# Moving the choice of the two best experts from stage A's turns into stage B's attention iterations

## The reference

```
x = x + layernorm(mamba(layernorm(x)))            # stage A: scan over 512 steps, 16 states, 512 channels
x = x + layernorm(ffn(layernorm(x)))              # the layer below
  ffn(src):   src = src + moe_attn(src); src = ln1(src)
              src = src + relu(src @ W1 + b1) @ W2 + b2; src = ln2(src)
  moe_attn(x): 16 heads of 64, 8 experts a head
      q, k = rope(x Wq[h]), rope(x Wk[h])
      gv   = gate(x, Wsel_v);  v = sum_e gv[h,s,e] * (x Wv[h,e])
      o    = softmax(q k' / 8) v
      go   = gate(x, Wsel_o);  out = sum_{h,e} go[h,s,e] * (o Wo[h,e])
  gate(x, Wsel): s = sigmoid(x Wsel); keep the 2 largest of the 8 experts of a head, the others are 0
```

## Time and profile before

| | us |
|---|---|
| median of 3 runs (4547.19 to 4552.66) | 4552.34 |
| the profiled execution, its own time | 4550.93 |
| its span in the profile | 4549.1 |
| TensorE busy | 3873.6 |
| VectorE busy | 3483.8 |
| GpSimd busy | 2705.4 |
| ScalarE busy | 2037.9 |

### The profile page before, as it was taken

One profiled execution on the slowest core, in us unless ns is written; L12 is line 12 of the kernel. 1 busy time (PEld: TensorE's weight loads), 2 busy tenths in 40 slices (PEclk: granted clock), 3 DMA queues, 4 the chain that ended last, 5 costly groups with the idle time before them and its releaser, 6 DMA issues. The chain is left out here.

```text
span 4549.1 us, 52321 instructions
## 1 busy us (share of the span) xinstructions
PE 3873.6 (85%) x16256; PEld 2698.3 (59%) x16256; DVE 3483.8 (77%) x3612; ACT 2037.9 (45%) x3761; POOL 2705.4 (59%) x1772
## 2 busy tenths in 40 slices
PE   6776766857666399999999999999999999999787
PEld 2232322323222277777777777777777777777676
DVE  5999999999999566666666666666666666666598
ACT  4544534435343144444444444444544544444443
POOL 2756656566476365665665666656655755665454
PEclk7786777868776699999999999999999999999899
DMA  1000000000000210010010000000100100000001
GB/s 37 0 10 14 10 19 19 9 14 9 23 9 10 76 62 14 14 39 9 14 39 9 32 21 14 35 14 14 39 9 14 39 9 14 19 14 9 34 28 42
DMA packets 48726, 97.83 MB, mean 22 GB/s; under 512 B 3570, under 2 KB 33138, under 8 KB 46228
## 3 DMA queue, kind: packets, MB, share of 16 engines
q1 hardware_dynamic: 47620, 92.94, 5.8%
q0 software_dynamic: 1040, 4.19, 0.2%
HBM read 80.34 MB, written 16.78 MB: 21 GB/s over the span
## 5 line engine op out<-in xcount | busy, mean ns | idle before, releaser
L723 DVE TENSOR_TENSOR_SCAN state<-dA,dBx 128x2048 f32<-128x2048 f32 x128 | 706.5, 5519 | 9.3 <-POOL y_part L309 4.3
L1015 POOL TENSOR_TENSOR qk_full<-vg 128x512 f32<-128x512 f32 x256 | 329.9, 1289 | 455.6 <-DVE vg L1330 455.6
L1230 ACT ACTIVATE prob<-ps_b,negmax 128x512 f32<-128x512 f32 x512 | 346.1, 687 | 549.3 <-DVE negmax L1336 549.3
L306 POOL TENSOR_TENSOR state<-state,c_copy 128x1024 f32<-128x1024 f32 x120 | 302.0, 2516 | 420.6 <-DVE state L723 420.6
L396 PE MATMUL ps_a<-xp_high,ident_r 33*128 33x512 f32 x256 | 163.3, 638 | 425.1 <-DVE dBx L713 399.7
L1330 DVE TENSOR_TENSOR vg<-ps_b,gates 128x1024 f32<-128x1024 f32 x256 | 313.6, 1225 | 255.0 <-PE ps_b L1072 251.2
L573 ACT ACTIVATE dA<-dt,a_neg 128x511 f32<-128x511 f32 x512 | 326.9, 711 | 398.3 <-DVE state L723 397.9
L1029 POOL TENSOR_TENSOR ogT_low<-prob,ogT_high 128x512 fp32r<-128x512 f32 x256 | 322.0, 1287 | 201.6 <-ACT ogT_high L1261 201.6
L1070 PE MATMUL ps_b<-wv_high,xT_high 128*128 128x512 f32 x1024 | 414.2, 404 | 0.0
L1070 PE MATMUL ps_b<-ogT_high,wo_high 128*128 128x512 f32 x1024 | 408.4, 399 | 0.0
L396 PEld LDWEIGHTS ps_a<-xp_high,ident_r 33*128 33x128 f32 x256 | 59.5, 232 | 583.2 <-DVE dBx L713 488.6
(11 more groups left out here) (232 smaller groups left out, 9658.0 us busy)
## 6 DMA issues: line engine op xcount, KB each, us to landing
xT<-xT_scratch SPq DMA_DIRECT2D x65, 512.0 KB, 3.2
wv<-in_wv SPq DMA_DIRECT2D x8, 1024.0 KB, 4.9
wo<-in_wo SPq DMA_DIRECT2D x8, 1024.0 KB, 6.9
x_in<-in_x SPq DMA_DIRECT2D x8, 512.0 KB, 4.6
x_a<-in_x SPq DMA_DIRECT2D x8, 512.0 KB, 5.3
x_scratch<-x_a SPq DMA_DIRECT2D x8, 512.0 KB, 2.9
xT_scratch<-x2T SPq DMA_DIRECT2D x8, 512.0 KB, 2.6
gates_scratch<-gate SPq DMA_DIRECT2D x8, 512.0 KB, 3.5
```

What stands on the lines that cost most here:

```text
L723: dve.tensor_tensor_scan(h[n % 2][:, :, :].rearrange("p c s -> p (c s)"), dA[n % 2][:, :, :].rearrange("p c s -> p (c s)"), dBx[n % 2][:, ...
L1015: pool.tensor_tensor(v4[:, at, :, :], vg[:, at, 0:4, :], vg[:, at, 4:8, :], ALU.add).then_inc(vsum_done, 1)
L1230: act.activation(prob[h][:, t, :], ps[:, score_bank(t) + h, :], ACT.Exp, bias=negmax[:, t, h:h + 1], accum_out=total[:, h, t:t + 1]).then_ ...
```

## The change

Stage A ends its tail with the sigmoid, which now writes the scores in the order of the pairs; SP stores these scores (512 KB a batch, as the gates before). The selection code, its GpSimd part and four buffers leave stage A.

In stage B, SP loads the scores of a pair for all batches. Each iteration chooses the two best for the iteration that follows it (the first one is served in `start()`). The groups are now the 16 of one pair in four row blocks, 128 scores a partition. VectorE keeps the four maxima (`tops`, 128 elements each). The equality tests become a difference and a test against zero on GpSimd, in four functions with 14 instructions of 128 elements: `rank_one` (3), `rank_two` (4), `rank_three` (3), `rank_four` (4). They stand in GpSimd's queue ahead of the first value sum, ahead of the second (behind `low_wqk` where there is one), behind the first `low_values`, and behind `low_x`. `tops` 0 to 3 stand in VectorE's queue behind `gate_values` 0, `maxima` 1, `maxima` 2 and `gate_values` 3. `gates` becomes a single buffer for one iteration, written by the last instruction of `rank_four`. `sem_inc(held, 1)` counts a semaphore that nobody reads; it stands between a wait and the instruction behind it.

```diff
                 sp.dma_start(d["xT"][bass.ds(c, 1)].rearrange("b p k s -> p b k s"), x2T[:, :, :].unsqueeze(1)).then_inc(x2T_stored, 16)
-                sp.wait_ge(gate_done, CREDIT + c * TT + TT)
-                sp.dma_start(d["gates"][:, :, bass.ds(c, 1)].rearrange("j p b t c -> p b j (t c)"),
-                             gate[:, :, :, :].rearrange("p j t c -> p j (t c)").unsqueeze(1)).then_inc(gate_stored, 16)
+                sp.wait_ge(sg_done, CREDIT + c * 2 + 2)
+                sp.dma_start(d["scores"][:, :, bass.ds(c, 1)].rearrange("j p b t c -> p b j (t c)"),
+                             sg[:, :, :, :].rearrange("p j t c -> p j (t c)").unsqueeze(1)).then_inc(sg_stored, 16)
 
...
-
-            def rank_picked(c, k):
-                pool.wait_ge(top_step, c * TOP + k + 2)
-                pool.tensor_tensor(groups(rank), groups(pick), first_g, ALU.mult).then_inc(top_step, 1)
...
-                    if n in (11, 13) and has_tail:
-                        rank_picked(i - 1, 3 * (n - 11))
...
-            rank_picked(NB - 1, 0)
-            rank_picked(NB - 1, 6)
...
-                    act.wait_ge(gate_done, CREDIT + c * TT)
+                    act.wait_ge(x1_done, CREDIT + c)
...
             def sigmoid(c, half):
+                if half == 0:
+                    act.wait_ge(sg_stored, CREDIT + c * 16)
                 act.wait_ge(sel_psum, c * 2 + half + 1)
-                act.activation(sg[:, half * S:(half + 1) * S], ps[:, TAIL[half], :], ACT.Sigmoid).then_inc(sg_done, 1)
+                act.activation(sg[:, :, 2 * half:2 * half + 2, :].rearrange("p j t c -> p t j c"),
+                               ps[:, TAIL[half], :].rearrange("p (t j c) -> p t j c", t=2, j=PAIRS), ACT.Sigmoid).then_inc(sg_done, 1)
...
-            def best_of(c, src, k):
-
-                step = c * TOP + k
-                if k == 0:
-                    dve.wait_ge(sg_done, CREDIT + c * 2 + 2)
-                else:
-                    dve.wait_ge(top_step, step)
-                dve.tensor_reduce(best[:, :], groups(src), AX.X, ALU.max).then_inc(top_step, 1)
-                dve.wait_ge(top_step, step + 1)
-                dve.tensor_tensor(groups(pick), groups(src), best_e, ALU.is_equal).then_inc(top_step, 1)
-
-            def first_of(c, src, k):
-
-                step = c * TOP + k
-                dve.wait_ge(top_step, step + 3)
-                dve.tensor_reduce(best[:, :], groups(rank), AX.X, ALU.max).then_inc(top_step, 1)
-                dve.wait_ge(top_step, step + 4)
-                dve.tensor_tensor(groups(pick), groups(rank), best_e, ALU.is_equal).then_inc(top_step, 1)
-                dve.wait_ge(top_step, step + 5)
-                dve.scalar_tensor_tensor(left[:, :], pick, -2.0, src, ALU.mult, ALU.add).then_inc(top_step, 1)
-
-            def gates(c):
-                dve.wait_ge(top_step, c * TOP + TOP)
-                dve.wait_ge(gate_stored, CREDIT + c * 16)
-                for t in range(TT):
-                    dve.scalar_tensor_tensor(gate[:, :, t, :], by_pair(left, t), 0.0, by_pair(sg, t),
-                                             ALU.is_lt, ALU.mult).then_inc(gate_done, 1)
...
-                        elif n == 11:
-                            best_of(c, sg[:, :], 0)
-                        elif n == 12:
-                            first_of(c, sg[:, :], 0)
-                        elif n == 13:
-                            best_of(c, left[:, :], 6)
-                        elif n == 14:
-                            first_of(c, left[:, :], 6)
-                        elif n == 15:
-                            gates(c)
...
-            best_of(last, sg[:, :], 0)
-            first_of(last, sg[:, :], 0)
-            best_of(last, left[:, :], 6)
-            first_of(last, left[:, :], 6)
-            gates(last)
...
-        gates = sb("gates", [P, NB * TT, GP])
+        scores_in = sb("scores", [P, NB * TT, GP])
+        gates = sb("gates", [P, TT, GP])
+        first = sb("first", [P, E])
+        GROUPS = TT * GP // E
+        top, top_first = sb("top", [P, GROUPS]), sb("top_first", [P, GROUPS])
+        far, hit, rank, left, picked = (sb(n, [P, GROUPS, E]) for n in ("far", "hit", "rank", "left", "picked"))
...
-                sp.wait_ge(gate_step, CREDIT + j * NB * GATE)
-                sp.dma_start(gates[:, :, :].unsqueeze(1), d["gates"][bass.ds(j, 1)].rearrange("j p b t c -> p j (b t) c")).then_inc(gates_loaded, 16)
...
+                if more:
+                    sp.wait_ge(gates_done, j * NB + NB)
+                    load_scores(j + 1)
                 sp.wait_ge(xT_low, CREDIT + j * NB + NB)
                 load_xT(0)
 
+            def load_scores(j):
+                sp.dma_start(scores_in[:, :, :].unsqueeze(1), d["scores"][bass.ds(j, 1)].rearrange("j p b t c -> p j (b t) c")).then_inc(scores_loaded, 16)
...
             sp.dma_start(vg[:, 0:2, :, :].rearrange("p t e n -> p (t e n)"), d["spread"]).then_inc(consts_loaded, 16)
             load_xT(0)
+            sp.dma_start(first[:, :], d["first"]).then_inc(scores_loaded, 16)
+            load_scores(0)
             load_weights(0)
...
+            def above(it, step, k, src):
+
+                pool.wait_ge(top_done, CREDIT + it * TOPS + k + 1)
+                pool.sem_inc(held, 1)
+                pool.tensor_tensor(far[:, :, :], src, each(top), ALU.subtract).then_inc(rank_step, 1)
+                pool.wait_ge(rank_step, step + 1)
+                pool.sem_inc(held, 1)
+                pool.tensor_scalar(hit[:, :, :], far[:, :, :], 0.0, None, ALU.is_ge).then_inc(rank_step, 1)
+                pool.wait_ge(rank_step, step + 2)
+                pool.tensor_tensor(rank[:, :, :], hit[:, :, :], first_g, ALU.mult).then_inc(rank_step, 1)
+
+            def first_above(it, step, k):
+
+                pool.wait_ge(top_done, CREDIT + it * TOPS + k + 1)
+                pool.tensor_tensor(far[:, :, :], rank[:, :, :], each(top_first), ALU.subtract).then_inc(rank_step, 1)
+                pool.wait_ge(rank_step, step + 1)
+                pool.sem_inc(held, 1)
+
+            def rank_one(it, b):
+                above(it, CREDIT + it * RANK, 0, grouped(scores_in[:, bass.ds(b * TT, TT), :]))
+
+            def rank_two(it, b):
+                step = CREDIT + it * RANK + 3
+                first_above(it, step, 1)
+                pool.tensor_scalar(picked[:, :, :], far[:, :, :], 0.0, None, ALU.is_ge).then_inc(rank_step, 1)
+                pool.wait_ge(rank_step, step + 2)
+                pool.sem_inc(held, 1)
+                pool.tensor_scalar(hit[:, :, :], picked[:, :, :], -2.0, None, ALU.mult).then_inc(rank_step, 1)
+                pool.wait_ge(rank_step, step + 3)
+                pool.sem_inc(held, 1)
+                pool.tensor_tensor(left[:, :, :], hit[:, :, :], grouped(scores_in[:, bass.ds(b * TT, TT), :]), ALU.add).then_inc(rank_step, 1)
+
+            def rank_three(it):
+                above(it, CREDIT + it * RANK + 7, 2, left[:, :, :])
+
+            def rank_four(it, b):
+                step = CREDIT + it * RANK + 10
+                first_above(it, step, 3)
+                pool.tensor_scalar(hit[:, :, :], far[:, :, :], 0.0, None, ALU.is_ge).then_inc(rank_step, 1)
+                pool.wait_ge(rank_step, step + 2)
+                pool.tensor_tensor(picked[:, :, :], picked[:, :, :], hit[:, :, :], ALU.add).then_inc(rank_step, 1)
+                pool.wait_ge(rank_step, step + 3)
+                pool.wait_ge(gate_step, CREDIT + it * GATE)
+                pool.sem_inc(held, 1)
+                pool.tensor_tensor(grouped(gates[:, :, :]), picked[:, :, :], grouped(scores_in[:, bass.ds(b * TT, TT), :]), ALU.mult).then_inc(gates_done, 1)
+
             def start():
+                rank_one(0, 0)
+                rank_two(0, 0)
+                rank_three(0)
+                rank_four(0, 0)
                 low_wqk(0)
...
                 pool.wait_ge(qk_low, it + 1)
+                coming, ahead = more or more_pairs, b + 1 if more else 0
+                if coming:
+                    rank_one(it + 1, ahead)
                 sum_values(it, 0, 0)
                 if more_pairs:
                     low_wqk(j + 1)
+                if coming:
+                    rank_two(it + 1, ahead)
                 sum_values(it, 0, 1)
                 low_values(it, 0)
+                if coming:
+                    rank_three(it + 1)
                 sum_values(it, 1, 0)
                 sum_values(it, 1, 1)
                 low_values(it, 1)
                 low_x(it + 1)
+                if coming:
+                    rank_four(it + 1, ahead)
...
-                    dve.wait_ge(gates_loaded, j * 16 + 16)
+                    dve.wait_ge(gates_done, it + 1)
...
+            def top_of(it, k, src):
+
+                step = CREDIT + it * RANK
+                dve.wait_ge(rank_step, step + (0, 3, 7, 10)[k])
+                dve.tensor_reduce((top_first if k % 2 else top)[:, :], src, AX.X, ALU.max).then_inc(top_done, 1)
+
```

(38 more changed lines are left out.)

15 lines of the change are left out of this document (7 added, 8 removed).

## The result

The changed kernel took 4659.7 us (median of 4 runs, 4657.4 to 4661.8) against 4552.5 before (4 runs): ratio 1.024, 95% interval 1.022 to 1.026, 107 us slower. The forecast was 4610 (range 4525 to 4680), slower. The profiled execution took 4659.97 us with a span of 4658.2, 109.1 more than the span before.

The account below looks back on a forecast made before the run. VectorE was taken to bound stage A and TensorE stage B. Stage A gives back 117 us; stage B costs 16 + 151 + 9 = 176, so +59 on 4550.9 gives 4610 us, range 4525 to 4680.

Parts of the forecast that it names:

- upper end of my sum: The total if each GpSimd test takes 0.46 us, as a two-input operation: 3.0 us an iteration, +98, 4649 us.
- dear tests: Rival: GpSimd tests take a slower path, 1.29 us each, adding 4.0 us an iteration; about 4865 us, chance 0.10.
- my two signs of being wrong: Stage B's iteration period grows by less than 1.5 us, or GpSimd tests take over 0.5 us.
- Tests on GpSimd, 0.3 us each: Stage B: price of a one-input test or scaling of 128 elements, put between 0.13 and 0.46 us.
- The `held` increments, 0.04 us each: Stage B: price of each of seven semaphore increments in GpSimd's queue up to the last value sum; ends nothing and 0.1.
- 2.4 us an iteration: Stage B: 5.0 us added before GpSimd's last value sum, less 2.6 idle, reaches TensorE; 63 iterations, 151 us.
- Pair ends, 1.3 us each: Stage B: in seven iterations the low part of `wqk` stands before rank two and finds its idle time used; 9 us.
- Hidden work: rank four and the maxima: Stage B: rank four's 2 us lie behind GpSimd's wait for ScalarE; delays of VectorE's later maxima lie inside the 2.4.
- 14.4 us a turn in stage A: Time each of turns 1 to 6 gives back without the selection, not VectorE's 20.5; six turns, 86 us.
- The start, 16 us: Stage B's first TensorE product comes 16 us late, behind the score load, the first choice (8.7 us) and `low_wqk`.
- hidden in stage B: Rival: GpSimd's delay before its last value sum doesn't reach TensorE, only the start is paid; 4450 us, chance 0.20.
- Stage A gives all: Rival: seven turns of stage A give VectorE's full 20.5 us each, 162 and not 117; 4565 us, chance 0.10.

Follow-up runs that it names:

- run 28: Not a run label: 28 of 48 ordinary iterations in the changed kernel with two more GpSimd products ahead of the last value sum; that kernel took 4760.3 us.

## Why the prediction was right, and where its numbers were off

The sign and the mechanism were right: stage A's gain is smaller than what GpSimd's queue costs TensorE in stage B. The signs that I named for it are in the trace: TensorE's waits of 1.27 us for VectorE's low probabilities and 1.10 us behind it, and ScalarE's second value copy waiting for GpSimd, 3.77 us now. The time was 50 us over the forecast, and that it still fell into the range is in part luck. 4659.7 lies above the upper end of my sum, 4649, and under the 4865 of dear tests; only the range's stretch to 4680 holds it. The terms also erred both ways: stage A gave 14.5 us more than forecast, stage B and what follows cost 65 more. And of my two signs of being wrong one came true, tests over 0.5 us. It speaks against my price of a test and not against the mechanism, since the period grew by 3.06 us. These terms were mis-sized.

- **Tests on GpSimd, 0.3 us each.** They took 0.53, above my upper end of 0.46. Four in the chain: +0.9 us an iteration. The bound was wrong in kind: I took a two-input operation as the upper end for a one-input one. The Trainium skill (GPSIMD Engine Reference, section 4.1, Engine selection) has one-input operations at roughly line rate; at this size they were the dearer ones in the trace, 530 ns against 408 to 459, and what an element costs them can't be read from one size. Its 12 cycles an element for branches (section 3.1), the reason beside "dear tests", don't show in these tests: the multiplication by -2, which compares nothing, took 534 ns, as the tests did.
- **The `held` increments, 0.04 us each.** The gap is 0.20 and not 0.08 where one stands: 0.12 each, at the five places in the chain where one follows another GpSimd operation. It isn't the kind of operation: the addition at L1017 shows 0.19 with one, that at L1027 0.08 without. The seven gaps come to 1.14 us for 0.85; some 0.13 comes back, since what follows each of the three groups starts 0.04 us before its last operation ends.
- **The far differences, 0.46 us.** They took 0.41, three of them: -0.15 us.
- **2.4 us an iteration.** Ten operations, their gaps and the first maximum come to 3 x 0.41 + 3 x 0.46 + 4 x 0.53 + 1.14 - 0.13 + 0.28 = 6.0 us, not 5.0. Against them the idle times gave back 1.96 and 1.46 - 0.74, 2.7 us as forecast. The last sum is 3.3 late, the period 3.06: 63 x 3.06 = 193 us for 151. That the chain has no slack was right: 0.90 of 1.0 us put into it went to the period, and none of the same work behind it.
- **Pair ends, 1.3 us each.** The two iterations around a change of pairs took 47.87 and 45.07 us against 43.62 and 39.72, 3.5 us beyond two ordinary losses: 7 x 3.5 = 24 for 9. I had costed the low part of `wqk` alone. The next iteration, where GpSimd starts with the low output weights, was a catch-up of 2 us before and has none now.
- **Hidden work: rank four and the maxima.** Right in ordinary iterations: GpSimd's waits for ScalarE ahead of the low outputs fell from 3.16 to 0.60 us, and freeing the maxima of their waits left the shortest period at 44.80. At pair ends the cover isn't there, as the two products behind the low outputs showed (+1.0 us each time).
- **14.4 us a turn in stage A.** Six turns gave (1341.21 - 216.97) - (1238.90 - 213.95) = 99.3, 16.5 each, between my 14.4 and VectorE's 20.5. Turn 0, from which I took the limit, had a delay of its own: the same stretch takes 68.0 us before and 228.41 - 162.96 = 65.4 after, though neither has a selection there. Before, GpSimd waited 7.06 us for ScalarE's copy of `xp` and began its weighing at 163.76; after, at 160.75. With 65.4 as the limit my subtraction gives 17.0. The last turn gave 9.4 where I put 12: VectorE now waits 3.71 us for GpSimd's last sum ahead of the skip term, the wait that I had named but priced at 2. The tail gave 19.8 for 19, and turn 0 another 3.0, by that same delay. These 3 us aren't the change's: in the ten kernels with the new stage A turn 1 begins between 213.95 and 217.66, before it was 216.97.
- **The start, 16 us.** 18.2: from stage A's last store to the landing of `sin` it is 23.0 us, for which I had 22.1, and the chain took 9.9 us for 8.7, tests again.
- **Last iteration and stage C, nothing.** 5.4 us, of which 3.7 stand without a choice too.

Of the rivals, "hidden in stage B" was a matter of place. Its 4450 would need a free chain; with the choice in GpSimd's idle slots the kernel took 4486, on the faster side of before. "Stage A gives all" was a third true (131.5 us in the traces, between my 117 and its 162) and too small to decide. "Dear tests" had the right direction, with 0.53 us for its 1.29.

## What to carry to other kernels

Work moved to an engine that is two thirds busy costs what its place in that engine's queue costs: ten small operations cost 3.1 us an iteration in front of the value sums, and all 14 nothing in the slots where the engine waits for others, so look at the timeline for the idle time in front of a wait before choosing where to insert. Price small operations by kind, one-input forms too, and bound an unknown one from above by more than the nearest sort. After the ordinary iterations are free, look at the irregular ones: here the changes of pairs kept 49 of the 59 us that remained.

## What the runs showed of the hardware that was not expected

**The granted clock fell in some of a set of equal iterations.** In the kernel with two more products in the chain, two iterations in a row had the same waits of TensorE (1.26 and 2.04 us, then 1.27 and 2.06, at the same places) and took 47.06 and 45.68 us. Windows of both, the stretch from 25 to 35 us after their begin:

```profile
1934.28:1939.28 5.00, 3.29 (x9) 2.63 (x10) 3.17 (x5) 3.16 (x7) 4.49 (x4) 0.75 0.00 0
1939.28:1944.28 5.00, 4.42 (x17) 3.26 (x16) 2.35 (x2) 2.46 (x5) 2.68 (x5) 0.90 0.34 105
...
1981.34:1986.34 5.00, 3.32 (x13) 2.48 (x14) 3.35 (x6) 3.13 (x7) 4.52 (x4) 1.00 0.00 0
1986.34:1991.34 5.00, 4.42 (x19) 3.30 (x18) 3.40 (x3) 2.67 (x5) 4.05 (x6) 1.00 0.30 105
```

At 0.75 and 0.90 part of each window ran at the 1.2 GHz level, just behind the 2 us wait; in the next iteration the same wait left the clock at 2.4 GHz. So 1.0 us of work in the chain cost 100 us and not 63 x 0.90 = 57. Of the 48 ordinary iterations of this run 28 had a mean clock of 0.96 and took 46.4 to 47.1 us, the others 1.00 and 45.7. The run with free maxima, in which TensorE's longest wait was 2.25 us, shows the same in 19 of 48. In the other nine kernels the longest wait in an ordinary iteration was 0.6 to 1.3 us, and there the clock stayed at 1.00 in all 48. That may be why the free maxima made the kernel slower: they joined two waits of 1.27 and 1.10 us to one of 2.25. What decides between two like iterations stays open.

**VectorE beside GpSimd.** An equality of 128 elements that reads two tiles took 1.96 us beside GpSimd's addition and 0.29 alone. The Trainium skill (GPSIMD Engine Reference, section 8, Key points) says that the two engines share interfaces to SBUF and that operations of VectorE with two inputs there are among those that contend; this trace agrees, and shows that the short one can be held till the long one ends. A maximum of VectorE, which reads one tile, took its usual 0.28 us beside the same addition; and where the equality began beside GpSimd's product instead, behind a change of pairs, it took 1.4 us and ended with that product.
